# Statistics of the next image's x: from VectorE's BN_STATS to sums and sums of squares on ScalarE

## The chip, the cores and the metric

One core of one Trainium2 chip runs the whole kernel. The metric is the time of one execution in microseconds (us), taken on the device. The kernel before takes 4247.38 us, the median of three runs (4243.71 to 4248.18).

## The reference

Input x has 8 images of 64x64 pixels and 256 channels. Two layers run one after the other, each as x + layer(group norm of x):

```
def _gn(v, G=32, eps=1e-5):            # groups of 8 channels, over all pixels
    m, s = mean, var over (pixels, the group's channels)
    return (g - m) / sqrt(s + eps)

x = x + L0(_gn(x))    # deformable conv (DCNv4): depthwise 3x3 -> 27 numbers per group and pixel
                      #   (18 offsets, 9 masks); value = x @ vp_w; 9 bilinear samples, masked sum; @ op_w
x = x + L1(_gn(x))    # binarised 3x3 conv, scaled by the box mean of |x| and by mean |kernel|
```

The change touches only how mean and variance of an image's x are found for the first group norm, for images 1 to 7.

## The kernel before, in words

Channels (or groups times blocks of rows) lie on the 128 partitions, pixels on the free axis. Function layer0 works image by image, n = 0 to 7, and each image in four steps, j = 0 to 3. A step takes four rows from each of four blocks of rows. In a step there are nine turns, k = 0 to 8, one for each tap of the 3x3 window. Images 1 to 6 are one hardware loop; image 0 and image 7 are written out.

Each engine has its own written order of work, and semaphores join them. In turn k:

- TensorE (PE) makes the offsets and the mask of tap k+2 (`offsets`, L746, 48 matmuls in three units), one unit of the next step's depthwise conv (`depthwise`, L718, k = 0 to 3), value units (L731), the transposes back and the projection of the step before (L759, L772), and the additions of the samples, which are transposes accumulated in PSUM (`add`, L791, two or three of 16 matmuls).
- ScalarE (ACT) turns the offsets into hat functions (`hats`, L577 to L591), takes the depthwise result from PSUM (`keep_depthwise`, L549), and normalises loaded rows (L542, L523; the most of it at k = 8).
- VectorE (DVE) multiplies hats (L921, L935), adds the products of taps 4, 5 and 8 (L963), and multiplies values by weights (`multiply`, L982), one pv buffer after the other. The additions of the five taps 1, 2, 3, 6 and 7 are DMAs with an add, issued by GpSimd (POOL, L470). There are four pv buffers, so DVE can be at most four products ahead of PE.

Statistics of the next image. While image n is worked on, half-channels of x of image n+1 are loaded into two buffers that are free at that time: `ahead[0]` is acc, loaded at k = 6 of steps 0 and 1, and `ahead[1]` is acc_t, loaded at the end of the turns of steps 0 and 1 (`load_ahead`, L453). One load is 128 partitions by 2048 pixels. DVE runs four BN_STATS of 512 over it (`sums_ahead`, L881): the first half at k = 7 of steps 0 and 1, the second half at k = 0 of steps 1 and 2. There are 4 such passes for each of 7 images, 28 in all.

In step 2 (`has_means`) the scales are made in parts at k = 0, 2, 4 and 6 (`scales_ahead`). At k = 0 DVE does, in this order: its products and multiplications of the turn, the last pass of sums, a wait until all four passes of the image are made, `statistics` of the layer's output (L992), and part 0 of the scales (L894, L896). PE opens turn k = 1 of step 2 with `group_mean` (L781), a matmul that waits for part 0, and only then goes on to the offsets of its turn. The lines that set this order on DVE and on PE stay as they are:

```
if k == 0 and has_means(n, j, NI):
    dve.wait_ge(sums_made, CH * CH * (n + 1))
...
if k in MEANS_AT and has_means(n, j, NI):
    group_mean(n, j, MEANS_AT.index(k), ...)     # PE: waits for gx_step
```

Of the kernel before, what the change touches and what calls it, by code (L numbers as in the profile page):

```python
# [8 lines left out]
ALU = mybir.AluOpType  # L9
ACT = mybir.ActivationFunctionType  # L10
AX_X = mybir.AxisListType.X

P = 128
H = W = 64
HW = H * W
C = 256
CH = C // P
# [24 lines left out]
EPS = 1e-5  # L42
# [186 lines left out]
def layer0(nc, x, zeros, w_dram, x2, consts, tables, mv2, reach, NI):  # L229


    with ExitStack() as ctx:
        sb = lambda name, shape, dt=F32: ctx.enter_context(nc.sbuf_tensor(name, shape, dt))
        psum = lambda name, shape: ctx.enter_context(nc.psum_tensor(name, shape, F32))
        sem = lambda name: ctx.enter_context(nc.semaphore(name))
# [20 lines left out]
        eye3 = sb("eye3", [P, 32])  # L256
        gx = sb("gx", [P, 2, CH])
        gx_tri = sb("gx_tri", [KROWS, CB, 2, CH])
        bs1 = sb("bs1", [P, CH, HW // 512, 6])
        mv1 = sb("mv1", [P, CH, 2])  # L260
        mean1 = sb("mean1", [P, CH])
        var1 = sb("var1", [P, CH])
# [30 lines left out]
        xres_added, stats2 = sem("xres_added"), sem("stats2")  # L293
        gn_kept = sem("gn_kept")
        x_ahead = [sem("x_ahead0"), sem("x_ahead1")]
        sums_made, gx_step = sem("sums_made"), sem("gx_step")
        gx_root = sem("gx_root")
        GX_STEPS = 11
        x2_stored, over_done, aggr2 = sem("x2_stored"), sem("over_done"), sem("aggr2")
        mv_kept = sem("mv_kept")  # L300
        WL = 16 * 10
# [27 lines left out]
        def has_next(n):  # L329
            return not (isinstance(n, int) and n == NI - 1)  # L330
# [22 lines left out]
        with nc.Block() as block:  # L353
# [144 lines left out]
            def _(act):  # L498

                def keep_scales(n, j):  # L500

                    if j == 0:
                        act.wait_ge(gx_step, gx_made(n))
                        act.wait_ge(gn_spread, 16 * 3 * CB * (n + 1))
                    nc.scalar.activation(gn[:, j % 2, :, :], gx[:, :, :], ACT.Copy).then_inc(gn_kept, 1)
                    nc.scalar.activation(gn_tri[:, j % 2, :, :], gx_tri[:, :, :, :].rearrange("p c s n -> p (c s) n"),
                                         ACT.Copy).then_inc(gn_kept, 1)
                    act.wait_ge(gn_kept, 2 * (STEPS * n + j + 1))
# [109 lines left out]
                def keep_mean(n, j, i):  # L618
# [2 lines left out]
                    nc.scalar.activation(gmean[:, i, :], ps_bg[:, bank(n, j, f"mean{i}", NI), 0:CH], ACT.Copy)\  # L621
                        .then_inc(bg_free, 2)

                keep_scales(0, 0)
                normalise(0, 0, 0)
                act.wait_ge(val_zero, 6)
# [20 lines left out]
                def step(n, j, first, last):  # L647
                    s = STEPS * n + j
                    n1, j1 = following(n, j)
                    n2, j2 = following(n1, j1)  # L650
                    more = not (isinstance(n, int) and n == NI - 1 and j >= STEPS - 2)

                    def place(name):
                        return unit(n, j, name, NI), bank(n, j, name, NI)

                    for k in range(TAPS):
                        if k in MEANS_AT and has_means(n, j, NI):
                            keep_mean(n, j, MEANS_AT.index(k))
                        if k == ROOT_AT and has_means(n, j, NI):
                            act.wait_ge(gx_step, GX_STEPS * n + 9)  # L660
                            nc.scalar.activation(var1[:, :], var1[:, :], ACT.Sqrt).then_inc(gx_root, 1)
                        if k == BACK_AT and not first:
                            if j in (1, 2) and has_next(n):
                                act.wait_ge(sums_made, CH * CH * n + CH * j)
                            summed(s - 1)
                        if k + 2 < TAPS:
                            hats(n, j, k + 2)
                        elif not last:
                            hats(n1, j1, k + 2 - TAPS)
                        if k in DW_AT and not last:  # L670
                            u = DW_AT.index(k)
                            keep_depthwise(j1, u, *place(f"dw{u}"))
                        if k in VALUES_AT and not last:
                            for i in shares(value_units(j1), VALUES_AT.index(k), len(VALUES_AT)):
                                keep_values(j1, i, *place(f"value{i}"), 2 * n1 + (1 if j1 == 0 else 2))
                        if k == BACK_AT and not first:
                            for u in range(BACK_UNITS):
                                keep_back(u, *place(f"back{u}"))
                        if k in PROJECT_AT and not first:
                            for u in range(PJ_UNITS):  # L680
                                if PROJECT_AT[u] == k:
                                    keep_x2(s - 1, u, *place(f"project{u}"))
                        if k in DW_AT[1:3] and not last:
                            normalise_tri(n1, j1, 1, DW_AT.index(k) - 1)
                        if k == 3 and not last:
                            normalise(n1, j1, 0)
                        if k == 6 and not last and j1 == 0:
                            normalise(n1, j1, 1)
                        if k == 8 and more:
                            keep_scales(n2, j2)  # L690
                            for qp in range(2):
                                normalise_tri(n2, j2, 0, qp)
# [10 lines left out]
            def _(pe):  # L703
# [72 lines left out]
                def group_mean(n, j, i, src):  # L776


                    pe.wait_ge(gx_step, GX_STEPS * n + (4, 8)[i])
                    pe.wait_ge(bg_free, unit(n, j, f"mean{i}", NI))  # L780
                    nc.tensor.matmul(ps_bg[:, bank(n, j, f"mean{i}", NI), 0:CH], consts["mean8"][:, :], src[:, :],  # L781
                                     start=True, stop=True).then_inc(bg_full, 2)
# [75 lines left out]
            def _(dve):  # L858
# [15 lines left out]
                nc.vector.memset(over_max[:, :], 0.0).then_inc(diag_made, 1)  # L874
                dve.wait_ge(diag_made, CH * CB * 3 + 1)

                def sums_ahead(n, j, half):

                    dve.wait_ge(x_ahead[half], 16 * (CH * n + j + 1))
                    for i in range(HW // 1024):  # L880
                        last = nc.vector.bn_stats(bs1[:, j, HW // 1024 * half + i, :], ahead[half][:, 512 * i:512 * i + 512])  # L881
                    last.then_inc(sums_made, 1)

                def scales_ahead(n, j, part):

                    def after(i, ins):
                        ins.then_inc(gx_step, 1)
                        dve.wait_ge(gx_step, GX_STEPS * n + 1 + i)

                    gm = gmean[:, 0, :]  # L890
                    if part == 0:

                        for h in range(CH):
                            nc.vector.bn_aggr(mv1[:, h, :], bs1[:, h, :, :]).then_inc(gx_step, 1)  # L894
                        dve.wait_ge(gx_step, GX_STEPS * n + 1 + CH)
                        after(3, nc.vector.tensor_copy(mean1[:, :], mv1[:, :, 0]))  # L896
                    elif part == 1:

                        dve.wait_ge(bg_free, unit(n, j, "mean0", NI) + 2)
                        after(4, nc.vector.tensor_tensor(mean1[:, :], mean1[:, :], gm, ALU.subtract))  # L900
                        after(5, nc.vector.tensor_tensor(mean1[:, :], mean1[:, :], mean1[:, :], ALU.mult))
                        after(6, nc.vector.tensor_tensor(var1[:, :], mv1[:, :, 1], mean1[:, :], ALU.add))
                        nc.vector.nop().then_inc(gx_step, 1)
                    elif part == 2:
                        dve.wait_ge(bg_free, unit(n, j, "mean1", NI) + 2)
                        after(8, nc.vector.tensor_scalar(var1[:, :], gmean[:, 1, :], EPS, None, ALU.add))
                    else:
                        dve.wait_ge(gx_root, n + 1)

                        dve.wait_ge(gn_kept, 2 * STEPS * (n + 1))  # L910
                        after(9, nc.vector.reciprocal(gx[:, 0, :], var1[:, :]))
                        after(10, nc.vector.scalar_tensor_tensor(out=gx[:, 1, :], in0=gm, scalar=-1.0,
                                                                 in1=gx[:, 0, :], op0=ALU.mult, op1=ALU.mult))

                        after(11, nc.vector.tensor_scalar(tables[:, 0:2, bass.ds((n + 1) * CH, CH)], gx[:, :, :], 1.0, None,
                                                          ALU.mult))

                def mask_rows(n, j, k):
# [94 lines left out]
                def step(n, j, first, last):  # L1013
# [7 lines left out]
                    for k in range(TAPS):  # L1021
# [10 lines left out]
                        elif not last:  # L1032
                            mask_rows(*following(n, j), 0)
                        multiply_next(k, 2)
                        if k == AHEAD_AT and j < CH and has_next(n):
                            sums_ahead(n, j, 0)
                        if k == 0 and j in (1, 2) and has_next(n):
                            sums_ahead(n, j - 1, 1)
                        if k == 0 and has_means(n, j, NI):
                            dve.wait_ge(sums_made, CH * CH * (n + 1))  # L1040
                        if k == 0 and not is_step(n, j, 0, 0) and not is_step(n, j, 0, 1):
# [697 lines left out]
```

## Time and profile before

| what | us |
|---|---|
| median of three runs | 4247.38 |
| the profiled execution's own time | 4246.04 |
| its span, first to last instruction | 4244.2 |
| PE, DVE, ACT busy in the span | 3872.8, 3561.1, 2423.4 |
| mean granted TensorE clock | 0.973 of full speed |

The span is what the trace covers; the run's own time is 1.8 us more. Busy time is the sum of an engine's instructions; a busy PE is not PE at its peak, since ends of matmuls are modelled. Layer 0 takes about the first 3520 us, layer 1 the rest.

### The profile page before, as it was taken

The page shows a single profiled execution, that of the slowest core. Times are in us where ns is not written, and L with a number is a line of the kernel's source. Part 1 is how long each engine was busy: PE and PEld are TensorE (multiplying, and loading weights), DVE is VectorE, ACT ScalarE, POOL GpSimd, SP SyncE. Part 2 cuts the span into 40 slices and gives each one's busy share as a digit, 9 for nine tenths or more (in the row PEclk, how much of TensorE's full clock was granted, in tenths as well). Part 3 has the DMA queues.
Part 4 walks back from the last instruction along what each step waited for, and adds up shares of the span by engine and source line. Part 5 has one row for each costly group of instructions (what it writes and reads, how often), then busy time and mean ns, then how long its engine had stood idle before and what let it go on. Part 6 is the DMA issues. An engine that isn't in the chain of part 4 may idle for free. (4 is left out here: it accounts for less than half of the span.)

```text
span 4244.2 us, 94584 instructions
## 1 busy us (share of the span) xinstructions
PE 3872.8 (91%) x38382; PEld 2480.9 (58%) x38382; DVE 3561.1 (84%) x2896; ACT 2423.4 (57%) x5027; POOL 569.8 (13%) x480
## 2 busy tenths in 40 slices
PE   3899999999999999999999999999999985888988
PEld 1466666666666666666666666666666663333333
DVE  2799899989998899899989998999899993556554
ACT  4666666666666666666666666666666622333332
POOL 0011111111111111111111111111111110222222
PEclk9999999999999999999999999999999996999999
DMA  4454455445544554555445544554454433222321
GB/s 129 108 115 100 101 126 123 99 103 119 120 100 104 120 119 99 109 123 119 99 101 125 124 99 101 121 129 99 100 106 104 79 57 133 89 90 90 136 92 60
DMA packets 308092, 453.20 MB, mean 107 GB/s; under 512 B 33456, under 2 KB 239024, under 8 KB 301872
## 3 DMA queue, kind: packets, MB, share of 16 engines
q0 software_dynamic: 95168, 197.15, 25.9%
q1 hardware_dynamic: 212464, 249.71, 19.4%
q8 instruction: 314, 5.14, 0.5%
q14 instruction: 146, 1.20, 0.1%
HBM read 245.38 MB, written 67.11 MB: 74 GB/s over the span
## 5 line engine op out<-in xcount | busy, mean ns | idle before, releaser
L982 DVE TENSOR_TENSOR pv<-val,wsum 128x2048 f32<-128x2048 f32 x800 | 1810.3, 2283 | 11.1 <-PE ps_add L791 11.0
L791 PEld LDWEIGHTS ps_add<-ident,pv 128*128 128x128 f32 x12800 | 1399.7, 142 | 325.7 <-issue 220.7
L791 PE MATMUL ps_add<-ident,pv 128*128 128x128 f32 x12800 | 1525.0, 275 | 39.5 <-DVE pv L982 31.0
L746 PE MATMUL ps_om<-xdw,omw 128*32 128x256 f32 x13824 | 884.4, 389 | 124.7 <-ACT hat L579 109.1
L746 PEld LDWEIGHTS ps_om<-xdw,omw 128*32 128x32 f32 x13824 | 395.0, 111 | 431.7 <-ACT hat L579 120.8
L470 POOL DMA_DIRECT2D wsum<-prod x192 | 226.0, 1255 | 2688.6 <-DVE wsum L935 2688.6
L577 ACT ACTIVATE hat<-ps_om,omb 128x256 f32<-128x256 f32 x576 | 275.4, 478 | 537.0 <-PE ps_om L746 537.0
L935 DVE TENSOR_TENSOR prod<-hat,mwy 128x1536 f32<-128x1536 f32 (+1 forms) x384 | 525.2, 1395 | 59.0 <-DMA wsum<-prod 42.5
L1530 PE MATMUL ps_c<-c_sgn,c_ksgn 128*128 128x512 bf16 x2304 | 518.7, 384 | 2.5 <-DVE c_res L1647 2.5
L542 ACT ACTIVATE tri<-tri,gn_tri 96x512 f32<-96x512 f32 (+3 forms) x812 | 473.5, 647 | 6.0 <-DMA tri<-in_zeros_dram 0.5
L921 DVE TENSOR_TENSOR mwy<-hat,msk 128x768 f32<-128x768 f32 x288 | 274.1, 952 | 223.7 <-ACT hat L591 223.5
L1530 PEld LDWEIGHTS ps_c<-c_sgn,c_ksgn 128*128 128x128 bf16 x2304 | 225.6, 98 | 311.2 <-issue 46.1
L718 PE MATMUL ps_bg<-tri,diag 128*32 128x512 f32 x3024 | 361.2, 613 | 0.0
L581 ACT ACTIVATE msk<-ps_om,omb 128x256 f32<-128x256 f32 x288 | 136.9, 475 | 377.4 <-PE ps_om L746 374.6
L1489 ACT ACTIVATE c_res<-c_res,c_bias,c_scale 128x512 f32<-128x512 f32 x128 | 103.1, 812 | 415.8 <-DVE c_res L1647 415.8
L731 PE MATMUL ps_bg<-win,vpw 128*32 128x256 f32 x5120 | 303.8, 383 | 37.2 <-DMA ident<-in_ident_dram 28.8
L579 ACT ACTIVATE hat<-ps_om,omb 128x256 f32<-128x256 f32 x576 | 280.8, 487 | 0.0
L578 ACT ACTIVATE hat<-ps_om,nomb 128x256 f32<-128x256 f32 x576 | 276.2, 480 | 0.0
L935 DVE TENSOR_TENSOR wsum<-hat,mwy 128x768 f32<-128x768 f32 (+2 forms) x288 | 256.6, 891 | 2.7 <-DVE pv L982 1.2
L731 PEld LDWEIGHTS ps_bg<-win,vpw 128*32 128x32 f32 x5120 | 167.1, 111 | 151.0 <-DMA ident<-in_ident_dram 28.9
L1647 DVE TENSOR_TENSOR c_res<-ps_c,c_box 128x512 f32<-128x512 f32 x128 | 87.1, 687 | 189.2 <-PE ps_c L1530 189.1
L1559 POOL TENSOR_TENSOR c_x<-c_x,c_res 128x512 f32<-128x512 f32 x128 | 170.2, 1334 | 542.5 <-ACT c_res L1489 542.5
(102 smaller groups left out, 2791.2 us busy)
## 6 DMA issues: line engine op xcount, KB each, us to landing
wsum<-prod POOLq DMA_DIRECT2D x160, 768.0 KB, 6.9
tri<-in_x_dram SPq DMA_DIRECT2D x725, 128.0 KB, 2.9
win<-in_x_dram SPq DMA_DIRECT2D x144, 256.0 KB, 3.3
xres<-in_x_dram POOLq DMA_DIRECT2D x128, 256.0 KB, 9.0
x<-xres SPq DMA_DIRECT2D x128, 256.0 KB, 4.1
c_x<-x SPq DMA_DIRECT2D x8, 4096.0 KB, 13.0
out_dram<-c_x SPq DMA_DIRECT2D x32, 1024.0 KB, 4.0
acc<-in_x_dram POOLq DMA_DIRECT2D x14, 1024.0 KB, 5.6
```

Of the source, the lines that this page charges most:

```text
L542: last = nc.scalar.activation(v, v, ACT.Identity, bias=gn_tri[p0:p1, j % 2, 2 * c + 1, h:h + 1], scale=gn_tri[p0:p1, j % 2, 2 * c, h:h + 1])
L577: nc.scalar.activation(hat[:, par, a, 1, :], d, ACT.Abs, bias=b).then_inc(abs_done, 1)
L578: nc.scalar.activation(hat[:, par, a, 0, :], d, ACT.Relu, bias=nb, scale=-1.0)
L579: nc.scalar.activation(hat[:, par, a, 2, :], d, ACT.Relu, bias=b).then_inc(om_free, 1)
L718: mm = nc.tensor.matmul(out[:, :, :, o0:o1], diag[:, h, c, kx, :], src, start=kx == 1, stop=kx == 2)
L731: mm = nc.tensor.matmul(ps_bg[G * q:G * q + G, par, ci * TOK:(ci + 1) * TOK], vpw[:, h, 2 * cp + ci, :], win[:, h, q, :, :], start=h == 0, ...
L746: mm = nc.tensor.matmul(ps_om[G * q:G * q + G, (par + i) % 2, 0:TOK], omw[:, h, comp, :], xdw[:, j % 2, h, q, :], start=h == 0, stop=h == ...
L791: mm = nc.tensor.matmul(ps_add[:, tb, c, :], pv[:, (j + uv) % PBUF, c, P * tb:P * tb + P], consts["ident"][:, :], start=uv == 0 and c % 4 ...
L921: nc.vector.tensor_tensor(mwy[:, :, :], hat[:, par, 1, :, :], msk[:, par, :].unsqueeze(1).to_broadcast([P, 3, TOK]), ALU.mult)\
L935: return nc.vector.tensor_tensor(dst, hat[:, par, 0, c:d, :].unsqueeze(1).to_broadcast(shape), mwy[:, a:b, :].unsqueeze(2).to_broadcast(sh ...
L982: nc.vector.tensor_tensor(pv[:, (j + uv) % PBUF, :, :].rearrange("p c (r w) -> p c r w", w=W), val[:, :, SR * j + u:SR * j + u + SR, v:v + ...
L1530: mm = nc.tensor.matmul(ps_c[u % BANKS][:, :, :], ksgn[:, h, k, P * oh:P * oh + P], sgn[:, b, h, 8 * t + ky:8 * t + ky + 8, kx:kx + W], st ...
```

## The change

`sums_ahead` moves from DVE's order to ACT's. ACT makes each pass of 2048 pixels by two instructions in place, Identity with bias and a sum, then Square with a sum. The bias is the negated first pixel of the channel (`pivot`), made by one more tiny ACTIVATE in a first half. The places have the same names as before (k = 7 of steps 0 and 1; k = 0 of steps 1 and 2), but now on ACT: after its hats, its copies out of PSUM and its normalising of that turn.

DVE keeps the wait for all sums at k = 0 of step 2, and its part 0 of the scales is five small instructions instead of two BN_AGGR and a copy. The additions of the five taps stay DMAs.

```diff
-                def sums_ahead(n, j, half):                       # was on DVE
-                    dve.wait_ge(x_ahead[half], 16 * (CH * n + j + 1))
-                    for i in range(HW // 1024):
-                        last = nc.vector.bn_stats(bs1[:, j, HW // 1024 * half + i, :], ahead[half][:, 512 * i:512 * i + 512])
-                    last.then_inc(sums_made, 1)
+                def sums_ahead(n, j, half):                       # now on ACT
+                    act.wait_ge(x_ahead[half], 16 * (CH * n + j + 1))
+                    v, i = ahead[half], 3 * (CH * n + j)
+                    if half == 0:
+                        nc.scalar.activation(pivot[:, j:j + 1], v[:, 0:1], ACT.Copy, scale=-1.0).then_inc(centred, 1)
+                        act.wait_ge(centred, i + 1)
+                    nc.scalar.activation(v, v, ACT.Identity, bias=pivot[:, j:j + 1],
+                                         accum_out=x_sums[:, half, j, 0:1]).then_inc(centred, 1)
+                    act.wait_ge(centred, i + 2 + half)
+                    nc.scalar.activation(v, v, ACT.Square, accum_out=x_sums[:, half, j, 1:2]).then_inc(sums_made, 1)
...
+                        if k == AHEAD_AT and j < CH and has_next(n):       # in ACT's step, ahead of k == 8
+                            sums_ahead(n, j, 0)
+                        if k == 0 and j in (1, 2) and has_next(n):
+                            sums_ahead(n, j - 1, 1)
...
-                        for h in range(CH):                       # DVE, scales_ahead, part 0
-                            nc.vector.bn_aggr(mv1[:, h, :], bs1[:, h, :, :]).then_inc(gx_step, 1)
-                        dve.wait_ge(gx_step, GX_STEPS * n + 1 + CH)
-                        after(3, nc.vector.tensor_copy(mean1[:, :], mv1[:, :, 0]))
+                        after(1, nc.vector.tensor_tensor(mv1[:, :, :], x_sums[:, 0, :, :], x_sums[:, 1, :, :], ALU.add))
+                        after(2, nc.vector.tensor_scalar(mv1[:, :, :], mv1[:, :, :], 1.0 / HW, None, ALU.mult))
+                        after(3, nc.vector.tensor_tensor(var1[:, :], mv1[:, :, 0], mv1[:, :, 0], ALU.mult))
+                        after(4, nc.vector.tensor_tensor(mv1[:, :, 1], mv1[:, :, 1], var1[:, :], ALU.subtract))
+                        after(5, nc.vector.tensor_tensor(mean1[:, :], mv1[:, :, 0], pivot[:, :], ALU.subtract))
...
-                        if k == AHEAD_AT and j < CH and has_next(n):       # DVE's step
-                            sums_ahead(n, j, 0)
-                        if k == 0 and j in (1, 2) and has_next(n):
-                            sums_ahead(n, j - 1, 1)
                         if k == 0 and has_means(n, j, NI):
                             dve.wait_ge(sums_made, CH * CH * (n + 1))
```

## Rows read from the trace of the kernel before

**Rows 1.** The page's busy time of each engine: us (share of span) xinstructions.

```profile
PE 3872.8 (91%) x38382; PEld 2480.9 (58%) x38382; DVE 3561.1 (84%) x2896; ACT 2423.4 (57%) x5027; POOL 569.8 (13%) x480
```

**Rows 2.** Busy time by stretch: step 1 of image 2, step 1 of image 7.

```profile
core 0: us, PE busy (x) PEld busy (x) DVE busy (x) ACT busy (x) POOL busy (x), PEclk, DMA share, GB/s
1034.40:1136.50 102.10, 99.21 (x1104) 67.89 (x1100) 101.01 (x79) 63.30 (x135) 13.12 (x12) 1.00 0.54 121
...
3166.70:3268.60 101.90, 100.44 (x1122) 68.77 (x1124) 96.47 (x72) 63.24 (x134) 11.99 (x10) 1.00 0.50 105
```

**Rows 3.** Timeline, image 2, step 1, k = 0: start, us, engine, line [idle before <-releaser].

```profile
1054.48 2.47 DVE L881 BATCH_NORM_STATS2 bs<-acc_t 128x6 f32<-128x512 f32 x4
...
1057.32 0.69 ACT L549 ACTIVATE xdw<-ps_bg,dwb 128x512 f32<-128x512 f32 x1 [0.71 <-PE ps_bg L718]
...
1061.96 0.48 ACT L577 ACTIVATE hat<-ps_om,omb 128x256 f32<-128x256 f32 x1 [3.95 <-PE ps_om L746]
...
1064.10 1.97 PE L791 MATMUL ps_add<-ident,pv 128*128 128x128 f32 x16 [1.34 <-DVE pv L982]
...
1065.99 1.07 PE L746 MATMUL ps_om<-xdw,omw 128*32 128x256 f32 x16
```

**Rows 4.** Timeline, image 7, step 1, k = 0: the same addition.

```profile
3197.21 1.97 PE L791 MATMUL ps_add<-ident,pv 128*128 128x128 f32 x16
```

**Rows 5.** Timeline, image 0: two additions of PE after sums on DVE.

```profile
187.46 2.96 PE L791 MATMUL ps_add<-ident,pv 128*128 128x128 f32 x16 [2.53 <-DVE pv L982]
...
212.24 1.97 PE L791 MATMUL ps_add<-ident,pv 128*128 128x128 f32 x16 [1.32 <-DVE pv L982]
```

**Rows 6.** ACT and DVE groups: line, operation, shapes xcount | busy, mean ns.

```profile
L1446 ACT ACTIVATE c_box<-c_box 128x2304 f32<-128x2304 f32 x2 | 4.1, 2114 | 13.3 <-DVE c_ksgn L1576 13.3
...
L591 ACT ACTIVATE hat<-hat 128x512 f32<-128x512 f32 x288 | 181.5, 630 | 9.1
L588 ACT ACTIVATE over<-hat,minus 128x512 bf16<-128x512 f32 x288 | 204.9, 712 | 0.0
L588 ACT ACTIVATION_READ_ACCUMULATOR over<-hat,minus 128x1 f32 x288 | 54.9, 190 | 0.0
...
L901 DVE TENSOR_TENSOR mean<-mean 128x2 f32<-128x2 f32 x7 | 1.1, 161 | 0.2
...
L214 ACT ACT_TABLE_LOAD x1 | 1.3, 1283 | 18.9 <-PEq L145 18.9
```

**Rows 7.** Timeline, image 2, step 0, around k = 7 and 8.

```profile
1040.09 0.48 ACT L577 ACTIVATE hat<-ps_om,omb 128x256 f32<-128x256 f32 x1 [3.80 <-PE ps_om L746]
...
1042.71 1.07 PE L746 MATMUL ps_om<-xdw,omw 128*32 128x256 f32 x16
```

**Rows 8.** Timeline, image 2, step 2, from k = 0 to k = 2.

```profile
1156.64 2.46 DVE L881 BATCH_NORM_STATS2 bs<-acc_t 128x6 f32<-128x512 f32 x4
...
1158.86 3.83 PE L718 MATMUL ps_bg<-tri,diag 128*32 128x512 f32 x24
...
1159.23 2.47 DVE L992 BATCH_NORM_STATS2 bs<-xres 128x6 f32<-128x512 f32 x4
...
1162.53 1.76 DVE L935 TENSOR_TENSOR prod<-hat,mwy 128x1536 f32<-128x1536 f32 x1
...
1162.76 0.69 ACT L549 ACTIVATE xdw<-ps_bg,dwb 128x512 f32<-128x512 f32 x1 [1.76 <-PE ps_bg L718]
...
1165.07 2.28 DVE L982 TENSOR_TENSOR pv<-val,wsum 128x2048 f32<-128x2048 f32 x1
...
1166.17 0.28 PE L781 MATMUL ps_bg<-mean 128*128 128x2 f32 x2
...
1168.24 1.97 PE L791 MATMUL ps_add<-ident,pv 128*128 128x128 f32 x16
...
1173.43 1.76 DVE L935 TENSOR_TENSOR prod<-hat,mwy 128x1536 f32<-128x1536 f32 x1 [0.80 <-DMA wsum<-prod]
```

**Rows 9.** Timeline, image 2, step 3, k = 0: PE after a long wait.

```profile
1265.65 1.94 PE L746 MATMUL ps_om<-xdw,omw 128*32 128x256 f32 x16 [6.82 <-ACT hat L579]
...
1267.36 4.18 PE L718 MATMUL ps_bg<-tri,diag 128*32 128x512 f32 x24
```

More of the change, by code:

```diff
@@ L258, in layer0 @@
         gx_tri = sb("gx_tri", [KROWS, CB, 2, CH])
-        bs1 = sb("bs1", [P, CH, HW // 512, 6])
+        pivot = sb("pivot", [P, CH])
+        x_sums = sb("x_sums", [P, 2, CH, 2])
         mv1 = sb("mv1", [P, CH, 2])
@@ L295, in layer0 @@
         x_ahead = [sem("x_ahead0"), sem("x_ahead1")]
-        sums_made, gx_step = sem("sums_made"), sem("gx_step")
+        sums_made, gx_step, centred = sem("sums_made"), sem("gx_step"), sem("centred")
         gx_root = sem("gx_root")
-        GX_STEPS = 11
+        GX_STEPS = 13
         x2_stored, over_done, aggr2 = sem("x2_stored"), sem("over_done"), sem("aggr2")
@@ L659, in step @@
                         if k == ROOT_AT and has_means(n, j, NI):
-                            act.wait_ge(gx_step, GX_STEPS * n + 9)
+                            act.wait_ge(gx_step, GX_STEPS * n + 11)
                             nc.scalar.activation(var1[:, :], var1[:, :], ACT.Sqrt).then_inc(gx_root, 1)
@@ L776, in group_mean @@
                 def group_mean(n, j, i, src):
-                    pe.wait_ge(gx_step, GX_STEPS * n + (4, 8)[i])
+                    pe.wait_ge(gx_step, GX_STEPS * n + (6, 10)[i])
                     pe.wait_ge(bg_free, unit(n, j, f"mean{i}", NI))
@@ L891, in scales_ahead @@
                     if part == 0:
-                        for h in range(CH):
-                            nc.vector.bn_aggr(mv1[:, h, :], bs1[:, h, :, :]).then_inc(gx_step, 1)
-                        dve.wait_ge(gx_step, GX_STEPS * n + 1 + CH)
-                        after(3, nc.vector.tensor_copy(mean1[:, :], mv1[:, :, 0]))
+                        after(1, nc.vector.tensor_tensor(mv1[:, :, :], x_sums[:, 0, :, :], x_sums[:, 1, :, :], ALU.add))
[3 more added lines that the diff above has]
+                        after(5, nc.vector.tensor_tensor(mean1[:, :], mv1[:, :, 0], pivot[:, :], ALU.subtract))
                     elif part == 1:
                         dve.wait_ge(bg_free, unit(n, j, "mean0", NI) + 2)
-                        after(4, nc.vector.tensor_tensor(mean1[:, :], mean1[:, :], gm, ALU.subtract))
-                        after(5, nc.vector.tensor_tensor(mean1[:, :], mean1[:, :], mean1[:, :], ALU.mult))
-                        after(6, nc.vector.tensor_tensor(var1[:, :], mv1[:, :, 1], mean1[:, :], ALU.add))
+                        after(6, nc.vector.tensor_tensor(mean1[:, :], mean1[:, :], gm, ALU.subtract))
+                        after(7, nc.vector.tensor_tensor(mean1[:, :], mean1[:, :], mean1[:, :], ALU.mult))
+                        after(8, nc.vector.tensor_tensor(var1[:, :], mv1[:, :, 1], mean1[:, :], ALU.add))
                         nc.vector.nop().then_inc(gx_step, 1)
@@ L905, in scales_ahead @@
                         dve.wait_ge(bg_free, unit(n, j, "mean1", NI) + 2)
-                        after(8, nc.vector.tensor_scalar(var1[:, :], gmean[:, 1, :], EPS, None, ALU.add))
+                        after(10, nc.vector.tensor_scalar(var1[:, :], gmean[:, 1, :], EPS, None, ALU.add))
                     else:
@@ L910, in scales_ahead @@
                         dve.wait_ge(gn_kept, 2 * STEPS * (n + 1))
-                        after(9, nc.vector.reciprocal(gx[:, 0, :], var1[:, :]))
-                        after(10, nc.vector.scalar_tensor_tensor(out=gx[:, 1, :], in0=gm, scalar=-1.0,
+                        after(11, nc.vector.reciprocal(gx[:, 0, :], var1[:, :]))
+                        after(12, nc.vector.scalar_tensor_tensor(out=gx[:, 1, :], in0=gm, scalar=-1.0,
                                                                  in1=gx[:, 0, :], op0=ALU.mult, op1=ALU.mult))
-                        after(11, nc.vector.tensor_scalar(tables[:, 0:2, bass.ds((n + 1) * CH, CH)], gx[:, :, :], 1.0, None,
+                        after(13, nc.vector.tensor_scalar(tables[:, 0:2, bass.ds((n + 1) * CH, CH)], gx[:, :, :], 1.0, None,
                                                           ALU.mult))
```

## The prediction

> **What bounds the kernel now.** I read the busy times first, then busy time by stretch for single steps of layer 0, then the timeline of PE, ACT and DVE at the turns where sums are made, and the same turns of image 7. Over the span PE is busy 91%, DVE 84%, ACT 57% [rows 1]. The average mixes both layers, so it doesn't say what a DVE instruction is worth. In step 1 of image 2 DVE is busy 101.01 of 102.10 us and PE 99.21 [rows 2]: both look like the bound. Image 7 separates them. It has no next image, so no sums: its step 1 holds 4.5 us less DVE work (96.47) and still takes 101.90 us, with PE at 100.44 [rows 2]. PE is the bound, an almost unbroken belt of matmuls in written order, and DVE's time counts only where PE waits for a product. So I look for PE's waits and how the change moves each of them.
>
> **DVE loses 28 passes: what that gives.** A pass is 2.47 us [rows 3], 28 of them are 69 us of DVE. Of this only PE's waits come back. At k = 0 of step 1 the pass starts at 1054.48, and PE's addition at 1064.10 had waited 1.34 us for a product [rows 3]. The same addition in image 7 has no such wait [rows 4]. That is 1.34 us for each of images 1 to 6, 8.0 us. Image 0 starts with DVE behind: waits of 2.53 and 1.32 us stand behind its first passes [rows 5]. Of the first at most the 2.47 us of the pass comes back, of the second all, 3.8 us. Gain: 8.0 + 3.8 = 11.8 us. Bounds: 8 us, if image 0 gives back nothing, and 14 us, if small later waits of DVE's go too.
>
> **What a pass costs on ACT.** No row has an ACTIVATE of 2048. Without a bias pointer 2304 elements take 2114 ns and 512 take 630 [rows 6], so (2114 - 630) / 1792 = 0.828 ns each, and 2048 take 2114 - 256 x 0.828 = 1902 ns: the Square. A bias pointer adds 712 - 630 = 82 ns [rows 6], which makes the Identity 1984. Each sum has a reading of the accumulator, 190 ns [rows 6]. Instructions overlap by some 0.1 us and hand over by a semaphore in about as much, so a pass takes 1.98 + 0.19 + 1.90 + 0.19 = about 4.25 us, and about 4.5 us in a first half with the pivot. Bounds: 3.9 us (two of 1.9 with hidden reads) and 5.0 us (10% slower with 0.3 us of hand-over). In all 14 x 4.5 + 14 x 4.25 = 123 us of ACT.
>
> **Three of four places are covered.** At k = 7 of steps 0 and 1 a first half of 4.5 us meets 3.80 us of ACT idle [rows 7]. ACT is 0.7 us late for its hats. PE needs the first of them at 1042.71, and the three hats from 1040.09 free that bank at about 1041.3; 1.4 us of margin takes the 0.7. Queued behind the pass on ACT are only these hats and then the copies and normalising of k = 8, whose lateness is absorbed by the next wait for PE. Cost 0; with 5.0 us it is 0 too; from 5.2 on PE would wait. At k = 0 of step 1 the 4.25 us stand against 3.95 us of idle, with 4 us from 1061.96 until PE wants the bank at 1065.99 [rows 3]: cost 0. Here the price of lost cover would be up to 14 x 0.7 us = 10 us, the top end of this term.
>
> **The fourth place is not: k = 0 of step 2.** Here DVE waits for all sums before it goes on, and until now it had made the last pass itself. It had done so from 1156.64 to 1159.1, then ran statistics at 1159.23, part 0, and the products of k = 1 at 1162.53 [rows 8]. ACT comes to the pass only after its copy of the depthwise unit, which waits for PE's unit and ends at 1162.76 + 0.69 = 1163.45 [rows 8]. The pass ends at 1163.4 + 4.2 = 1167.6. DVE, which is at the wait from about 1156.6 or earlier, stands for 11 us. What is queued behind its wait is all that follows:
> - statistics, 2.4 us: until 1170.0;
> - part 0, now five dependent instructions of 0.16 us each [rows 6] at a pitch of some 0.2 us: until 1171.1. PE's group mean, which ran at 1166.17 without waiting, starts about 5 us late, and the offsets and additions of PE stand behind it;
> - the products of k = 1 start at 1171.1 instead of 1162.53, 8.6 us late. The product that PE adds at 1168.24 was ready at 1165.07 + 2.28 = 1167.35 [rows 8]; it is now ready at 1175.9. So PE's addition is 1175.95 - 1168.24 = 7.7 us late. This holds the 5 us of the group mean.
> - the products of k = 2 wait for the DMA of tap 1: 1173.43 is 10.9 us after 1162.53 [rows 8], so they start at 1182.0, 8.6 us late against PE's 7.7. The difference of 0.9 comes out where DVE's lead over PE is smaller than that; I take half, 0.4 us.
> - after its wait of 6.82 us PE's next 16 offsets take 1.94 us and the depthwise unit 4.18, against 1.07 [rows 3] and 3.83 [rows 8] elsewhere [rows 9]. I read this as a lower granted clock for a while after a long idle. Most of it falls here into the second half of the wait, between the group mean and the addition. I take 0.5 us, between 0 and 2.
>
> Nothing later gives this back: PE's next long wait, 6.82 us at the end of the step, is for ACT's normalising [rows 9], which follows PE's own turns and moves with them. Loss: 7.7 + 0.4 + 0.5 = 8.6 us an image, 60 us in seven. Bounds: 7.4 (pass of 3.9, nothing for the last two terms) and 11.4 (pass of 5.0, 0.9 and 2.0), 52 to 80 us.
>
> The Trainium skill speaks for the change at one point. Perfetto Trace Analysis, section Optimizing Scalar/DVE Operations, says that if DVE is saturated, moving work to ScalarE may make sense. DVE at 101.01 of 102.10 us looks saturated, and by that rule up to 69 us would go; image 7 speaks against it. It is a rival below.
>
> **Sum.** 4246.0 (the profiled execution's own time; its span is 4244.2) - 11.8 + 60 = 4294. The median of the runs is 1.3 us above the profiled run: 4295. With the bounds, 52 - 14 = +38 and 80 + 10 - 8 = +82 us; of the second I think the half-way point, 4312, is already rare. The forecast's own range is 4285 to 4312.
>
> **Rivals.**
> 1. ACT's last pass is done before it matters, and only the gain is left: 4247.4 - 11.8 = 4235. For it: ACT is 43% idle, and DVE gets 69 us of air. Against: the order on ACT puts the pass behind the depthwise copy at 1163.45. It decides at the end of that pass: products of k = 1 may start at 1163.4 at the latest without delaying PE's addition, so the sums would have to be made by about 1160; up to 1161.6 (1.7 us late, 11.8 / 7) the change still wins. I have 1167.6. Chance 8%.
> 2. DVE is the bound after all: its 69 us come off, 4178. Its busy share in step 1 speaks for it, the 101.90 us of image 7's step 1 against [rows 2]. The skill's rule above belongs here. Chance 2%.
> 3. The delay is only the group mean's: PE loses the 5 us before it, and the addition isn't late, since DVE, lighter by its passes, catches up: 7 x 5 - 11.8 = +23, 4270. Against: DVE can't pass its wait, so it can't have run ahead. Chance 6%. A still smaller loss near 1.7 us an image, within 8 us of no change: 4%.
> 4. Square lies in another table than the square root. The only table load in the trace is 1283 ns [rows 6], and Relu, Abs, Copy and Identity ran without one beside Sqrt; Square is not in it. A load before each Square and one behind, 2.6 us a pass: at k = 7 4.5 + 2.6 is 3.3 us over the idle time, less 1.4 of margin, 1.9 us x 14 = 27 us, and 1.3 us in each last pass, 9 us: 4331. With two loads an image it is 4295 to 4304. Chance of the dear form 5%.
>
> In the Trainium skill, ScalarE: Activation LUTs, section What ACT_TABLE_LOAD costs, a switch of sets is put at about 2.66 us with its drain; by that rival 4 would be twice as dear. No run here shows a switch.
>
> **How the numbers follow.** Forecast 75%, the rivals 8, 2, 6 + 4 and 5%. A change can be told from none here from about 0.2%, 8 us. Faster is rivals 1 and 2: 0.10. Same: 0.04. Slower is the rest: 0.86. The range reaches to rival 3 at the low end and beyond the forecast's own at the high end: 4270 to 4318; rival 1, rival 2 and the dear form of 4 lie outside.
>
> **What would show it.** In the timeline of step 2 DVE's L992 should start about 8.4 us later after PE's first depthwise unit than now, with an idle of 11 us or more before it released by ACT's Square; the group mean should have some 5 us of PE idle before it, and the next addition another 1 to 3 us for DVE's pv. Step 1's addition should lose its 1.34 us. ACT busy should rise by 123 us, DVE's fall by 69. The passes at k = 7 should leave PE without a new wait for hats. Wrong would be: L992 starting less than 3 us later; step 0 shorter by 2 us (rival 2); a table load beside Square (rival 4); or new waits of PE for hats at k = 8.

## The result, and the profile after

The changed kernel takes 4290.0 us, the median of four runs (4285.86 to 4293.0), against 4246.3 for the kernel before beside it. The ratio is 1.0103 with a 95% interval of 1.0085 to 1.012: slower by 44 us. Run again on another chip it took 4291.8 us, 1.0107 (1.0091 to 1.0122). Forecast were 4295 us and a range of 4270 to 4318.

The profiled run took 4285.86 us, 39.8 us more than the profiled run before; its page begins as follows (us, share of the span, instructions):

```profile
PE 3881.1 (91%) x38382; PEld 2481.3 (58%) x38382; DVE 3496.6 (82%) x2798; ACT 2536.9 (59%) x5153; POOL 569.9 (13%) x480
```

Against [rows 1] VectorE is 64.5 us less busy and ScalarE 113.5 us more; 69 and 123 were forecast. Neither number says what the time did. That has to be found on TensorE: its busy time rose by 8.3 us (3872.8 to 3881.1) and the span by 39.7, so some 31 us are more idle time and 8 us are the same matmuls taking longer.

To see where they lie I cut layer 0 at the start of each step's first depthwise unit on TensorE (the first `ps_bg<-tri,diag` of each step in the timeline). Sums over the steps of images 0 to 6, in us, worked out from those starts:

| kernel (profile) | steps 1 | steps 2 | steps 3 |
|---|---|---|---|
| before | 729.7 | 757.3 | 798.8 |
| changed | 720.1 | 811.5 | 793.1 |
| changed, second profile | 719.9 | 813.5 | 793.7 |

Step 0 of images 1 to 6 is 100.1 us in all of them. Steps 1 became 9.6 us shorter, steps 2 54.3 us longer, 7.75 each. Steps 3 hold the hardware loop's jump back, where TensorE stands 2 to 4 us without anything to wait for; their 5.7 us are taken up again below, under the sum.

Step 1 of image 2 by stretch, in the columns of [rows 2]:

```profile
1042.60:1144.90 102.30, 100.76 (x1126) 68.99 (x1128) 96.28 (x71) 71.51 (x144) 13.12 (x12) 1.00 0.55 124
```

DVE's busy time fell from 101.01 to 96.28 us, and the stretch, which is cut by DVE's work, did not get shorter: 102.30 us against 102.10. By TensorE's cuts the same step went from 104.3 to 103.1 us. DVE looked saturated, and 4.7 us less work on it were worth 1.3 us.

Timeline of the changed kernel, image 2, from k = 0 of step 2 on; it answers to [rows 8]:

```profile
1168.17 3.63 PE L735 MATMUL ps_bg<-tri,diag 128*32 128x512 f32 x24
...
1171.87 0.69 ACT L550 ACTIVATE xdw<-ps_bg,dwb 128x512 f32<-128x512 f32 x1 [1.57 <-PE ps_bg L735]
...
1172.46 2.00 ACT L632 ACTIVATE acc_t<-acc_t,pivot 128x2048 f32<-128x2048 f32 x1
1174.36 0.18 ACT L632 ACTIVATION_READ_ACCUMULATOR acc_t<-acc_t,pivot 128x1 f32 x1
1174.58 1.91 ACT L635 ACTIVATE acc_t<-acc_t 128x2048 f32<-128x2048 f32 x1
1176.39 0.19 ACT L635 ACTIVATION_READ_ACCUMULATOR acc_t<-acc_t 128x1 f32 x1
1176.70 2.47 DVE L1003 BATCH_NORM_STATS2 bs<-xres 128x6 f32<-128x512 f32 x4 [11.40 <-ACT acc_t L635]
...
1179.86 0.16 DVE L907 TENSOR_TENSOR mean<-mv,pivot 128x2 f32<-128x2 f32 x1
1180.15 1.76 DVE L946 TENSOR_TENSOR prod<-hat,mwy 128x1536 f32<-128x1536 f32 x1
1180.27 0.56 PE L798 MATMUL ps_bg<-mean 128*128 128x2 f32 x2 [4.82 <-DVE mean L907]
1180.75 3.33 PE L763 MATMUL ps_om<-xdw,omw 128*32 128x256 f32 x32
...
1182.69 2.28 DVE L993 TENSOR_TENSOR pv<-val,wsum 128x2048 f32<-128x2048 f32 x1
...
1185.03 1.97 PE L808 MATMUL ps_add<-ident,pv 128*128 128x128 f32 x16 [0.95 <-DVE pv L993]
```

Read it from the top: PE's unit, ScalarE's copy of it, the two instructions of the pass, then DVE, released after 11.40 us, then statistics, part 0 of the scales, and the group mean after 4.82 us of PE idle. PE's addition starts 16.86 us after the depthwise unit (1185.03 - 1168.17); before it was 9.38 (1168.24 - 1158.86). The difference is 7.5 us. The offsets between the group mean and the addition took 3.33 us in place of 1.93, because the granted clock was at the lower of its two levels (0.50 of full speed, 1.2 GHz, from 1181 to 1183; 0.66 as the mean of 1180 to 1185). That delay lies inside the wait for the product: without it PE would only have waited longer than 0.95 us.

The waits of all seven images, from the list of waits (us in total, times, longest). The seventh wait for the group mean, image 0's, stands there without a releaser (issue, 4.6 us):

```profile
DVE bs L1003 <- ACT acc_t L635: 80.9, 7, 11.9
PE ps_bg L798 <- DVE mean L907: 28.9, 6, 4.8
```

The covered places: timeline of the changed kernel, image 2: the end of a first half at k = 7 of step 0, and the addition at k = 0 of step 1. They answer to [rows 7] and [rows 3]:

```profile
1050.94 0.18 ACT L635 ACTIVATION_READ_ACCUMULATOR acc<-acc 128x1 f32 x1
1051.03 0.46 ACT L578 ACTIVATE hat<-ps_om,omb 128x256 f32<-128x256 f32 x1
...
1051.74 0.47 ACT L580 ACTIVATE hat<-ps_om,omb 128x256 f32<-128x256 f32 x1
...
1053.28 1.07 PE L763 MATMUL ps_om<-xdw,omw 128*32 128x256 f32 x16
```

```profile
1073.24 1.97 PE L808 MATMUL ps_add<-ident,pv 128*128 128x128 f32 x16
```

The hats start straight behind the pass and free the bank at 1052.21; PE wants it at 1053.28 and doesn't wait: 1.07 us of margin. The addition of step 1 has lost its 1.34 us of wait.

ScalarE's instructions by shape (busy us, mean ns):

```profile
L632 ACT ACTIVATE acc_t<-acc_t,pivot 128x2048 f32<-128x2048 f32 x14 | 28.0, 2000 | 0.0
L635 ACT ACTIVATE acc_t<-acc_t 128x2048 f32<-128x2048 f32 x14 | 26.8, 1912 | 0.4
...
L214 ACT ACT_TABLE_LOAD x1 | 1.3, 1283 | 19.1 <-PEq L145 19.1
```

### The profile page after: what moved, and what is told of

Its sections match the earlier page's. It is cut to its first block and busy times, and to the rows that moved or that the text cites. A ratio compares the mean times of both kernels' runs of the same rounds, so it can differ in the third digit from the quotient of the medians.

```text
span 4283.9 us, 94666 instructions
## 1 busy us (share of the span) xinstructions
PE 3881.1 (91%) x38382; PEld 2481.3 (58%) x38382; DVE 3496.6 (82%) x2798; ACT 2536.9 (59%) x5153; POOL 569.9 (13%) x480
## 5 line engine op out<-in xcount | busy, mean ns | idle before, releaser
L763 PE MATMUL ps_om<-xdw,omw 128*32 128x256 f32 x13824 | 896.5, 394 | 127.3 <-ACT hat L580 112.6
L946 DVE TENSOR_TENSOR prod<-hat,mwy 128x1536 f32<-128x1536 f32 (+1 forms) x384 | 525.9, 1397 | 82.2 <-DMA wsum<-prod 65.5
L789 PE MATMUL ps_bg<-acc_t,opw 128*128 128x512 f32 x512 | 240.3, 610 | 1.8 <-ACT val L566 1.1
```

What stands on the lines that cost most here:

```text
L763: mm = nc.tensor.matmul(ps_om[G * q:G * q + G, (par + i) % 2, 0:TOK], omw[:, h, comp, :], xdw[:, j % 2, h, q, :], start=h == 0, stop=h == ...
L946: return nc.vector.tensor_tensor(dst, hat[:, par, 0, c:d, :].unsqueeze(1).to_broadcast(shape), mwy[:, a:b, :].unsqueeze(2).to_broadcast(sh ...
```

## The experiments

**1. No dependence on the last pass.** The work on ScalarE stays, the wait for its last pass goes; the scales are made from the first half of each channel's pixels only.

```diff
-                            dve.wait_ge(sums_made, CH * CH * (n + 1))
+                            dve.wait_ge(sums_made, CH * CH * n + 3)
-  after(1, nc.vector.tensor_tensor(mv1[:, :, :], x_sums[:, 0, :, :], x_sums[:, 1, :, :], ALU.add))
+  after(1, nc.vector.tensor_tensor(mv1[:, :, :], x_sums[:, 0, :, :], x_sums[:, 0, :, :], ALU.add))
```

> The changed kernel with all its ScalarE passes, but VectorE waits at k = 0 of step 2 only for three of the four passes, and part 0 of the scales takes the first half's sums twice in place of the second half's: the scales come from half of the pixels. Theory A (the wait for the last pass is the loss, 7.75 us in each of seven step 2): 4290 - 54 = 4236 us, 0.25% below the kernel before; step 2 back to 108 us, no idle of TensorE before its group mean. Rival B (123 us more work on ScalarE make the hats late, the wait only shows it): 4285 to 4295 us.

Measured: 4241.5 us, ratio 0.9985 (0.9975 to 0.9995); 4236 was expected. Timeline, image 2, step 2: the group mean doesn't wait, and the pass runs on until 1166.6, behind it.

```profile
1157.49 4.33 PE L735 MATMUL ps_bg<-tri,diag 128*32 128x512 f32 x24
...
1164.61 1.91 ACT L635 ACTIVATE acc_t<-acc_t 128x2048 f32<-128x2048 f32 x1
1165.30 0.28 PE L798 MATMUL ps_bg<-mean 128*128 128x2 f32 x2
...
1167.38 1.97 PE L808 MATMUL ps_add<-ident,pv 128*128 128x128 f32 x16
```

Steps 2 sum to 760.6 us, 51 less than in the changed kernel, with all of ScalarE's new work still there; 3 of the 5 us that are missing to 4236 are in these steps, which took 757.3 us before the change. Theory A holds, rival B falls.

**2. Statistics ahead of the wait.** Two statements of DVE's order change places.

```diff
-                        if k == 0 and has_means(n, j, NI):
-                            dve.wait_ge(sums_made, CH * CH * (n + 1))
                         if k == 0 and not is_step(n, j, 0, 0) and not is_step(n, j, 0, 1):
                             statistics(*previous(*previous(n, j)))
+                        if k == 0 and has_means(n, j, NI):
+                            dve.wait_ge(sums_made, CH * CH * (n + 1))
```

> The changed kernel with statistics of the output (2.4 us on VectorE) ahead of the wait for the sums at k = 0 of step 2. Theory A: what stands behind the wait is shorter by 2.4 us, so each step 2 is 2.4 us shorter: 4290 - 17 = 4273 us, ratio to before 1.006; TensorE idles 2.4 us before the group mean instead of 4.8. Rival B: no change, 4290 us, 1.010.

Measured: 4286.5 us, 1.0093 (1.0076 to 1.011), about four us less instead of 17. The group mean's wait did fall as expected, to 2.4 us (14.1 us in six images, 28.9 in the changed kernel). So the time misses what the trace shows. The same kernel again, beside the changed one:

> The changed kernel itself, beside the next three on one chip. 4290 us, ratio to before 1.010. Step 1 102.3 to 103.1 us, step 2 of images 1 to 6 116.0 to 116.3.

> Statistics ahead of the wait, once more: the first time the steps 2 were each 2.0 us shorter in the trace, but the time only 4 us. Theory A: 14 us less than the changed kernel on this chip, about 4276 us; if the shorter step 2 is given back somewhere in each image (step 3 longer), 4 us less, 4286.

Measured on that chip: the changed kernel 4291.8 us, 1.0107 (1.0091 to 1.0122); statistics first 4291.4 us, 1.0105 (1.009 to 1.0121). No gain in the medians; the two profiled runs differ by 3.5 us. In the trace of layer 0 there is more: steps 2 sum to 802.1 us, 11.4 less than beside it, and the first convolution of layer 1 starts 10.6 us earlier (3621.9 against 3632.5). Layer 1 then loses 7 of them: from there to the end it takes 664.3 us against 657.2. Timeline of statistics first, second profile, layer 1:

```profile
3971.00 0.69 DVE L1614 TENSOR_TENSOR c_box<-c_box,c_hsum 128x512 f32<-128x512 f32 x1
3982.44 2.49 DVE L1654 TENSOR_TENSOR c_res<-ps_c,c_box 128x512 f32<-128x512 f32 x4 [10.74 <-issue]
3983.16 2.93 ACT L1496 ACTIVATE c_res<-c_res,c_bias,c_scale 128x512 f32<-128x512 f32 x4 [18.69 <-DVE c_res L1654]
3983.19 6.99 PE L1537 MATMUL ps_c<-c_sgn,c_ksgn 128*128 128x512 bf16 x19 [4.24 <-DVE c_res L1654]
```

DVE stands 10.74 us with nothing to wait for that the profile shows, PE waits 4.24 us for it, and that image takes 89 us instead of 82. Both profiles of statistics first have this idle once (10.6 and 10.7 us); no profile of the changed kernel or of another order has it.

**3. Does that idle hang on where the instructions lie?** First an empty instruction behind the wait, then 64 of them in the branch between the layers that is never taken, with and without statistics first.

```diff
                             dve.wait_ge(sums_made, CH * CH * (n + 1))
+                            nc.vector.nop()
```

```diff
                 with dve.If(dve.value_load(flag[0:1, 0:1], min_val=0, max_val=1) > 0):
                     link(nc.vector.memset(rows[:, :, :, :], 0.0))
+                    for _ in range(64):
+                        nc.vector.nop()
```

> Statistics ahead of the wait, with an empty instruction on VectorE behind the wait, so that VectorE's program is a few instructions longer up to layer 1. In both profiles of statistics first, layer 0 was 10 to 11 us shorter than in the changed kernel, and layer 1 had one idle of 10.6 us on VectorE that waits for nothing (issue), which no other profile has. If that idle hangs on where the instructions lie, it goes, and theory A's gain shows in the time: 11 to 14 us less than the changed kernel, ratio to before 1.0075 (4281 us). If it belongs to the order of the work, it stays: 1.0100 to 1.0105.

> Statistics ahead of the wait, with 64 empty instructions on VectorE in the branch between the layers that is never taken: the same work, but VectorE's instructions of layer 1 lie 64 places further. If the idle of 10.6 us in layer 1 hangs on where the instructions lie, it goes and the kernel takes 4279 to 4281 us, ratio 1.0075; if it belongs to the order of the work in layer 0, it stays, 1.0100 to 1.0105.

> The changed kernel with the same 64 empty instructions in the branch not taken. Its layer 1 has no such idle now: 4290 us, ratio 1.0105. If an idle near 10 us comes up here, the place of instructions alone can cost it: 1.012 to 1.013.

Measured: 1.0101 (1.0085 to 1.0117) with one empty instruction, 1.0101 (1.0084 to 1.0118) with 64, 1.0103 (1.0087 to 1.012) for the changed kernel with 64. The idle stayed in both (10.6 and 10.1 us) and didn't come up in the third. So a shift of this size doesn't move it; it comes with the program that has statistics first. What is shown is that it takes about 7 us in layer 1, and that the time alone would have led to a wrong reading of the order in layer 0.

Its cause stays open, but the traces hold a lead. The profile's page lists a DMA queue that carries instructions (packets, MB, share of 16 engines); first statistics first, second profile, then the changed kernel beside it:

```profile
q14 instruction: 156, 1.28, 0.1%
q14 instruction: 152, 1.24, 0.1%
```

All four profiles with the idle have 156 packets, all ten others 146 to 152. Two packets of this queue fall into the idle from 3971.7 to 3982.4, while the data queue takes 82% of the DMA engines' time; at the same place of the changed kernel (3978 to 3994) the data are loaded too and the queue moves nothing. That fits a VectorE that waits for its next instructions, but which engine the packets are for isn't in the trace, and no experiment tested it.

**4. The scales one turn later.** The wait and part 0 go to k = 1, the group means to k = 2 and 4, the other parts and the root one turn later too. The work is the same.

```diff
-    ... "dw" (0,) + "mean" (0, 0) + "dw" (1, 2) + "mean" (1, 1) + "dw" (3,) ...
+    ... "dw" (0, 1) + "mean" (0, 0) + "dw" (2, 3) + "mean" (1, 1) ...
-        MEANS_AT = [1, 3]
-        SCALES_AT = [0, 2, 4, 6]
-        ROOT_AT = 5
+        MEANS_AT = [2, 4]
+        SCALES_AT = [1, 3, 5, 7]
+        ROOT_AT = 6
-                        if k == 0 and has_means(n, j, NI):
+                        if k == 1 and has_means(n, j, NI):
                             dve.wait_ge(sums_made, CH * CH * (n + 1))
```

> The changed kernel with everything of the next scales one turn later in step 2: the wait and part 0 at k = 1, the group means at k = 2 and 4, the root at 6, the last part at 7. Statistics stay at k = 0. Theory A: the last pass ends 8.6 us after the first depthwise unit, VectorE comes to the wait about 10 us after it, so nothing waits: 4290 - 54 = 4236 us, ratio to before 0.9975, scales right. Rival B: 4285 to 4295 us. A third way: the last part at k = 7 makes the spread of the scales late for ScalarE's k = 8, and a wait of some 5 us an image moves there: 4270 us.

Measured: 4241.4 us, 0.9988 (0.9978 to 0.9997), with steps 2 at 761.3 us; 4236 was expected. The third way, 4270 us, is out. Timeline, image 2, step 2:

```profile
1155.77 4.43 PE L735 MATMUL ps_bg<-tri,diag 128*32 128x512 f32 x24
...
1164.80 0.19 ACT L635 ACTIVATION_READ_ACCUMULATOR acc_t<-acc_t 128x1 f32 x1
1165.64 1.97 PE L808 MATMUL ps_add<-ident,pv 128*128 128x128 f32 x16
1165.81 0.16 DVE L903 TENSOR_TENSOR mv<-x_sums 128x4 f32<-128x4 f32 x1
...
1174.64 0.28 PE L798 MATMUL ps_bg<-mean 128*128 128x2 f32 x2
```

The pass ends at 1164.99, DVE reads the sums at 1165.81 without a wait, and the addition comes 9.87 us after the depthwise unit.

> The kernel before (sums on VectorE) with the same move by one turn of parts, group means and root. Theory A: nothing waited there, so nothing comes back: 4244 to 4249 us, ratio 1.000 within 0.0007. If the later place is good for itself (another order of units on TensorE), it is 4236 or less, and the third run says nothing for A.

The same move in the kernel before: 4248.5 us, 0.9999 (0.999 to 1.0009). The later place is worth nothing by itself; what it gives is the wait. The two kernels together show what the change itself is worth without its wait: 0.9988 against 0.9999. The two intervals overlap, so by the times alone this small gain isn't certain; the steps 1 say the same, 718.0 us against 728.8 in the kernel before with the same move.

> The scales one turn later, once more, for a narrower interval: 0.9988 of the kernel before, between 0.998 and 0.9995. By the steps of its first trace: step 1 1.4 us shorter than before in seven images (10 us), step 2 0.5 us longer (4 us), so 6 us less in all, 4241 us.

Measured: 4240.2 us, 0.998 (0.9971 to 0.999). This version beats the kernel before by 0.1 to 0.2% and the changed kernel by 1.2%.

**5. The last pass earlier.** On ScalarE the pass goes ahead of the copy of the depthwise unit.

```diff
+                        if k == 0 and j == 2 and has_next(n):
+                            sums_ahead(n, 1, 1)
                         if k in DW_AT and not last:
                             u = DW_AT.index(k)
                             keep_depthwise(j1, u, *place(f"dw{u}"))
...
-                        if k == 0 and j in (1, 2) and has_next(n):
-                            sums_ahead(n, j - 1, 1)
+                        if k == 0 and j == 1 and has_next(n):
+                            sums_ahead(n, 0, 1)
```

> The changed kernel with the last pass in step 2 ahead of the copy of the depthwise unit on ScalarE instead of behind it; the copy comes 4.2 us after the hats. In the trace of the changed kernel the hats end at 1170.3 and the pass begins at 1172.46, so the sums are made 2.2 us earlier. Theory A (what counts is when the last pass ends): step 2 2.2 us shorter, 15 us in all, 4275 us. If the copy of the depthwise unit is then late for TensorE: no gain or a loss, 4290 or more.

Measured: 4282.8 us, 1.0084 (1.007 to 1.0098), 9 us less than the changed kernel on that chip, where 15 were expected. Timeline, image 2:

```profile
1166.26 3.96 PE L737 MATMUL ps_bg<-tri,diag 128*32 128x512 f32 x24
...
1172.23 0.18 ACT L635 ACTIVATION_READ_ACCUMULATOR acc_t<-acc_t 128x1 f32 x1
...
1176.10 0.35 PE L800 MATMUL ps_bg<-mean 128*128 128x2 f32 x2 [2.24 <-DVE mean L909]
...
1180.87 1.97 PE L810 MATMUL ps_add<-ident,pv 128*128 128x128 f32 x16 [2.55 <-DVE pv L995]
```

The sums are made 6.2 us after the depthwise unit, 2.3 earlier than in the changed kernel, and the addition comes at 14.6 instead of 16.9: up to there the gain is passed on whole. The group mean's wait fell by 2.6 us and the product's rose by 1.6: both hang on one chain on DVE, and only its end counts. The step as a whole gained 2.7 us in images 1 and 2 and 0.8 in images 3 to 6. Stretches of the same kernel, the same turns behind the addition in image 2 and image 4 (columns as in [rows 2]):

```profile
1182.00:1190.00 8.00, 8.00 (x84) 5.31 (x85) 8.00 (x5) 5.31 (x9) 1.07 (x1) 1.00 0.68 142
...
2046.00:2054.00 8.00, 8.00 (x67) 4.71 (x66) 8.00 (x5) 3.69 (x7) 1.04 (x1) 0.79 0.48 91
```

In image 4, after nearly the same two waits (2.47 and 2.55 us, the second until 2044.9), the mean granted clock was 0.79 there: 0.50 from 2046 to 2049 and back at 1.00 from 2050. PE did 67 matmuls in 8 us instead of 84. In image 2 it stayed at 1.00 throughout. From the addition to k = 4, where no wait is recorded, it needed 34.9 us instead of 33.3. So 1.6 us of the gain were given back there as a stretch at the lower of the clock's two levels. The steps 2 of images 3 to 6 are all 1.6 us longer than those of images 1 and 2 (115.3 against 113.7). That is the greater part of what is missing to the 15 us.

**6. How much cover is there at k = 7?** Two more copies in place of 1.9 us before each first half.

```diff
                     if half == 0:
+                        nc.scalar.activation(v, v, ACT.Copy).then_inc(centred, 1)
+                        act.wait_ge(centred, i - 1)
+                        nc.scalar.activation(v, v, ACT.Copy).then_inc(centred, 1)
+                        act.wait_ge(centred, i)
```

> The changed kernel with two more copies in place of 2048 elements (1.9 us each) before each first-half pass at k = 7 of steps 0 and 1. In the changed kernel ScalarE frees the offsets' bank at 1052.21 and TensorE wants it at 1053.28: 1.07 us of margin. Cover theory: 3.8 - 1.07 = 2.7 us of new wait of TensorE for the hats in each of 14 places, 38 us, 4328 us, step 0 102.8 us. If 40% of idle on ScalarE were free to use (the busy share decides): 4290 us.

Measured: 4339.6 us, 1.0221 (1.0207 to 1.0235), 48 us above the changed kernel; the cover theory had said 38. Timeline, image 2, step 0:

```profile
1063.12 0.19 ACT L639 ACTIVATION_READ_ACCUMULATOR acc<-acc 128x1 f32 x1
...
1064.45 1.07 PE L767 MATMUL ps_om<-xdw,omw 128*32 128x256 f32 x16 [2.81 <-ACT hat L580]
1065.34 3.39 PE L752 MATMUL ps_bg<-win,vpw 128*32 128x256 f32 x32
```

The wait is 2.81 us where the margin had given 2.7. The value unit behind it took 3.39 us where 1.91 is usual, with the granted clock at 0.50 from 1066 to 1069. So a place cost 4.2 us in step 0 (104.3 us) and 3.7 in step 1, not 2.7; steps 2 were 0.9 us shorter each. ScalarE was 40% idle all the while.

## Why the prediction was right, point by point

**The bound.** Right. TensorE's belt sets the step, DVE's busy share doesn't (experiments 1 and 4: with 64 us less DVE work the medians are 5.2 to 5.5 us below the kernel before). Rival 2 is out. The Trainium skill (Perfetto Trace Analysis, Optimizing Scalar/DVE Operations) says that offloading to ScalarE may make sense if DVE is saturated; here DVE was busy for 99% of a step, and that alone didn't make the move pay. The reading of image 7 was too strong, though. The 101.90 and 102.10 us are cut by DVE's work. By TensorE's cuts image 7's step 1 took 102.5 us and image 2's 104.3, so DVE's passes did cost something there, of which the 1.34 us of the addition are the greater part.

**The gain, 11.8 us.** Measured 9.6 in steps 1, 1.37 an image, as the 1.34 of step 1's addition said. Image 0's term was mis-sized: of 3.8 us only 1.4 came, in its step 1. The first pass is gone from DVE, but DVE then waits for the DMA of a tap's addition. Timeline of the changed kernel, image 0, k = 8:

```profile
183.09 2.36 DVE L946 TENSOR_TENSOR prod<-hat,mwy 128x1536 f32<-128x1536 f32 x2 [2.17 <-DMA wsum<-prod]
...
188.32 1.97 PE L808 MATMUL ps_add<-ident,pv 128*128 128x128 f32 x16 [2.42 <-DVE pv L993]
```

PE's wait of 2.53 us [rows 5] is still 2.42. Over the kernel DVE's waits for these DMAs rose from 42.5 to 65.5 us: 23 us, a third of the 69 that ScalarE took off DVE, went there, unseen by the time. In two further profiles of the changed kernel it was more, 71.5 and 71.8 us.

**The pass on ScalarE, 4.25 us.** Right: Identity 2000 ns and Square 1912, forecast 1984 and 1902; the last pass from 1172.46 to 1176.58 is 4.1 us.

**Three covered places at no cost.** Right: step 0 stays at 100.1 us, and the margin left at k = 7 is 1.07 us, forecast 0.7. Experiment 6 shows that cover was a matter of this margin and not of ScalarE's idle share. The price of lost cover, though, I had put at the wait alone; the lower clock behind it added half as much again in step 0.

**The fourth place, 8.6 us an image.** The mechanism is shown by experiments 1, 4 and 5: take the dependence away, or its date, and the loss goes. Steps 2 lost 7.75 us each, 54 us, not 60. The chain by its links, forecast and measured: group mean 5 and 4.8 us late; addition 7.7 and 7.5 us late. The two terms behind it, 0.4 for DVE's lag and 0.5 for the clock, were together 0.3. The clock's loss of 1.7 us (0.3 on the group mean, 1.4 on the offsets) lay inside the wait for the product, and I still counted 0.5 on top. The rows for that term were also read too low: the 3.83 us taken as a usual depthwise unit [rows 8] itself stand behind a wait of 2.93 us at the lower level, and other depthwise units of 24 matmuls take 2.73 us (at 1054.52 and 1171.03). After the wait of 6.82 us the unit of 4.18 [rows 9] was thus 1.45 us longer than usual, not 0.35; the granted clock was at 0.50 from 1264 to 1270.

**The sum.** +54.3 in steps 2, -9.6 in steps 1, +1.6 in step 0 of image 0, -5.7 in steps 3 and -0.7 ahead of them give the 39.9 us between the profiles' last marks, where +48 was forecast. By the runs it is +44. The terms for image 0 and ahead of it belong to one profile; in the second they are -0.1 and +1.7.

The steps 3 don't belong to one profile. "Nothing later gives this back" was wrong by about 5 us: three profiles of the changed kernel (the third is that with 64 empty instructions, experiment 3) have 793.1 to 793.7 us there, five of kernels without the wait (the kernel before, its late version, experiments 1 and 4) 797.2 to 799.3. The time at the lower level of the clock, summed from the granted clock in stretches of 1 us, is 31 to 32 us in the steps 3 of the first three and 39 to 42 in those of the five. Experiments 5 and 6 lie between, at 795.0 and 794.6; with statistics first steps 3 take 795.2 to 801.0 us, so it doesn't go with every late step 2, and why it is so stays open. The forecast was thus 6 us too high for steps 2 and 5 too high for steps 3, against 2 us of gain that image 0 didn't bring: some 9 us in all. That it missed the median by 5 us only is in part luck, since runs differ: between the last marks, two profiles of the changed kernel lie 39.9 and 43.4 us above the kernel before.

**The table load** (rival 4): there is one, as before, so Square lies with the others. Rivals 1 and 3 would have needed the sums made by about 1160, or an addition on time; the addition was late by 7.5 us.

What stays open is the idle of 10 us in layer 1 of the kernels with statistics first, which neither one empty instruction nor 64 moved, and the 5 us of steps 3.

## What to carry to other kernels

Before work goes from a busy engine to an idle one, ask two things of the trace: does the bound engine ever wait for the busy one at that place, and who reads the result first. Here the busy engine's time was worth 14% of what was taken off it (9.6 of 69 us). The last of the four passes had the wait for it 0.1 us behind it and its reader 2.5 us behind it on the old engine; on the new one it stood at the end of a queue, 4.1 us of work that began only behind a copy that waited for TensorE. A result that changes engines needs its reader moved too: one turn later, at no cost, turned a loss of 1% into a gain of 0.1 to 0.2%.

## What the runs showed of the hardware that was not expected

- After a wait of TensorE of 2.8 us the next value unit took 3.39 us instead of 1.91, and after 4.82 us the offsets 3.33 instead of 1.93. In both places the granted clock was at 0.50. Behind two waits of about 2.5 us the clock of another kernel (experiment 5) fell to that level in image 4, from about 1 us after the second wait until 2049, worth 1.6 us, and not in image 2.
- A program that differs in the order of two statements in layer 0 had an idle of 10.1 to 10.7 us on VectorE in layer 1, once per run, in four profiles of four; no other program of this case had it. The same four profiles show 156 packets of the instruction queue, all others 146 to 152.
